# Edge stages of a graph network: the edge product kept as fp32 in SBUF and summed by fp32 matmuls, in place of high and low fp32r parts

## The reference

```
m   = x[src] * rel[edge_type]                       # one row of 256 values for each of 106250 edges
agg = segment_sum((m @ W_half) / deg[dst], dst)     # W_in for the first half of the edges, W_out for the second
x   = x + res * tanh(agg + x @ W_loop + b)
```

## Time and profile before

| | us |
|---|---|
| timed, median of 3 | 2799.92 |
| profiled execution, first to last instruction (its own time; the page lists no other) | 3183.3 |
| edge stage 0 (67 to 1306) | 1239 |
| edge stage 1 (1459 to 2686) | 1227 |
| PE busy | 2759.1 (87%) |
| DVE busy | 2303.9 (72%) |
| ACT busy | 1865.5 (59%) |
| POOL busy | 1952.0 (61%) |

### The profile page before, as it was taken

The page is one execution under the profiler, slowest core; times in us unless marked ns, Lnnn a source line. Parts: engine busy times, 40 slices in busy tenths (PEclk is TensorE's granted clock), DMA queues, the critical chain, the costliest instruction groups (busy, mean ns, idle before and its releaser), DMA issues. The chain is left out here.

```text
span 3183.3 us, 55393 instructions
## 1 busy us (share of the span) xinstructions
PE 2759.1 (87%) x20688; PEld 2587.3 (81%) x20688; DVE 2303.9 (72%) x3258; ACT 1865.5 (59%) x3179; POOL 1952.0 (61%) x2129
## 2 busy tenths in 40 slices
PE   4888888888888888797888888888888887997998
PEld 3888888888888888796877887878777786997998
DVE  6777777777677777896777777777777776995665
ACT  6556665555555555585555555555555554785444
POOL 6666666666666666455666666666666664892223
PEclk9999989999999999899999999999999999998999
DMA  8333333333333333353333333333333333452221
GB/s 259 119 90 89 89 89 90 89 89 90 88 89 90 90 88 90 92 164 104 90 90 90 89 90 92 88 90 90 89 89 92 88 90 98 136 158 90 69 67 64
DMA packets 162458, 312.57 MB, mean 98 GB/s; under 512 B 34061, under 2 KB 95309, under 8 KB 162229
## 3 DMA queue, kind: packets, MB, share of 16 engines
q0 software_dynamic: 79872, 218.21, 23.8%
q1 hardware_dynamic: 81120, 89.89, 8.8%
q10 hardware_dynamic: 1237, 1.41, 0.2%
HBM read 263.90 MB, written 45.48 MB: 97 GB/s over the span
## 5 line engine op out<-in xcount | busy, mean ns | idle before, releaser
L740 PE MATMUL edge_rg<-edge_rel_hi,edge_hot 128*128 128x256 f32 x6656 | 1551.7, 293 | 86.6 <-issue 63.0
L740 PE MATMUL edge_rg<-edge_rel_lo,edge_hot 128*128 128x256 f32 x4992 | 1312.3, 289 | 60.0 <-issue 58.9
L740 PEld LDWEIGHTS edge_rg<-edge_rel_hi,edge_hot 128*128 128x128 f32 x6656 | 1219.6, 197 | 143.7 <-issue 92.2
L548 ACT ACTIVATE edge_hot<-edge_typ,minus_type 128x512 fp32r<-128x512 f32 x832 | 526.8, 685 | 935.9 <-DMA dense_prev<-emb_t 383.9
L740 PEld LDWEIGHTS edge_rg<-edge_rel_lo,edge_hot 128*128 128x128 f32 x4992 | 983.1, 197 | 70.0 <-issue 68.5
L623 DVE TENSOR_TENSOR edge_m_lo<-edge_rg,edge_m_hi 128x1024 fp32r<-128x1024 f32 x416 | 509.3, 1224 | 241.3 <-ACT edge_m_hi L541 127.7
L604 DVE TENSOR_SCALAR edge_hot<-edge_typ,type_of 128x512 fp32r<-128x512 f32 x832 | 582.3, 741 | 12.4 <-ACT edge_hot L548 8.7
L753 PE MATMUL edge_small<-edge_m_hi,edge_sel 128*128 128x258 f32 x1664 | 458.1, 306 | 96.3 <-DVE edge_m_lo L623 90.7
L530 POOL DMA_INDIRECT edge_xg<-emb,src x416 | 399.0, 959 | 225.9 <-issue 96.2
L530 POOL DMA_INDIRECT work<-h,src x416 | 400.7, 963 | 221.9 <-issue 101.9
L530 POOL DMA_INDIRECT edge_xg<-h,src x416 | 400.2, 962 | 216.2 <-issue 102.8
(11 more groups left out here) (183 smaller groups left out, 3933.9 us busy)
## 6 DMA issues: line engine op xcount, KB each, us to landing
work<-emb,src POOLq DMA_INDIRECT x416
edge_xg<-emb,src POOLq DMA_INDIRECT x416
work<-h,src POOLq DMA_INDIRECT x416
edge_xg<-h,src POOLq DMA_INDIRECT x416
set_x_rows<-in_x SPq DMA_DIRECT2D x25, 256.0 KB, 3.9
emb<-set_e_rows SPq DMA_DIRECT2D x25, 256.0 KB, 2.9
emb_t<-acc SPq DMA_DIRECT2D x5, 1280.0 KB
dense_prev<-emb_t SPq DMA_DIRECT2D x25, 256.0 KB, 2.7
```

Of the source, the lines that this page charges most:

```text
L548: act.activation(hot[:, q % 2, c], typ[q % 2][:], ACT.Abs, bias=K["minus_type"][:, c:c + 1]).then_inc(distances, 1)
L740: ins = pe.matmul(rg[q % 2][:, t, :], hot[:, q % 2, c, t * P:(t + 1) * P], part[:, c, :], start=(c == 0 and part is rel_hi), stop=(c == FULL))
```

## The change

The product is written by DVE to SBUF as fp32, into `m`, a ring of four groups; `rg` in PSUM is only read. `m_hi`, `m_lo`, `high` and `low` are gone, and with them `hi_done` and `lo_done`. The selection matrix is fp32 in place of fp32r. PE sums with one fp32 matmul per tile, of 257 columns (256 and one of ones), where it had one of 258 and one of 256 in fp32r. PE's sums wait for `selected`, which DVE sets with the selection matrix, behind the product. The unused way `long()` is changed likewise.

```diff
-        m_hi = s.sb("m_hi", [P, 2, GROUP, DIM + 2], F32R)
-        m_lo = s.sb("m_lo", [P, 2, GROUP, DIM], F32R)
-        sel = s.sb("sel", [P, GROUPS_IN_RING, GROUP * WIN + P - WIN], F32R)
-        sums_sb = s.sb("sums_sb", [WIN, 2, DIM + 2])
+        m = s.sb("m", [P, GROUPS_IN_RING, GROUP, DIM + 1])
+        sel = s.sb("sel", [P, GROUPS_IN_RING, GROUP * WIN + P - WIN])
+        sums_sb = s.sb("sums_sb", [WIN, 2, DIM + 1])
...
-            def high(g, q, i):
-                act.wait_ge(messages, g + 1)
-                act.copy(m_hi[:, q % 2, :, 0:DIM], rg[q % 2][:]).then_inc(hi_done, 1)
...
-                over_groups(act, (0, later(distance)), (2, high), (0, later(one_hot)), (3, copy_sums), (0, clear_one))
+                over_groups(act, (0, later(distance)), (0, later(one_hot)), (3, copy_sums), (0, clear_one))
...
-                dve.tensor_tensor(rg[q % 2][:], xg[q // 2][:, at, :], rg[q % 2][:], ALU.mult).then_inc(messages, 1)
-            def low(g, q, i):
-                dve.wait_ge(hi_done, g + 1)
-                dve.tensor_tensor(m_lo[:, q % 2], rg[q % 2][:], m_hi[:, q % 2, :, 0:DIM].bitcast(F32),
-                                  ALU.subtract).then_inc(lo_done, 1)
+                dve.tensor_tensor(m[:, q, :, 0:DIM], xg[q // 2][:, at, :], rg[q % 2][:], ALU.mult).then_inc(messages, 1)
...
                     select(sel_at(q, 0, GROUP * WIN).rearrange("p (t n) -> p t n", n=WIN),
-                           K["dst_rel"][:, ds(GROUP * g, GROUP)])
+                           K["dst_rel"][:, ds(GROUP * g, GROUP)]).then_inc(selected, 1)
...
-                over_groups(dve, (2, message), (2, one_window), (4, add_window), (2, low), (0, one_hot_later))
+                over_groups(dve, (2, message), (2, one_window), (4, add_window), (0, one_hot_later))
...
-            dve.memset(m_hi[:, :, :, DIM:].bitcast(F32), 0.0).then_inc(filled, 1)
-            dve.wait_ge(filled, 2)
-            dve.memset(m_hi[:, :, :, DIM:DIM + 1].bitcast(F32), 1.0).then_inc(filled, 1)
+            dve.memset(m[:, :, :, DIM:], 1.0).then_inc(filled, 1)
...
-                    pe.wait_ge(lo_done, g + 1)
+                    pe.wait_ge(selected, g + 1)
                     for t in range(GROUP):
-                        lhs = sel_at(q, t, P)
-                        pe.matmul(sums[q // 2][:], lhs, m_hi[:, q % 2, t, :], start=(q % 2 == 0 and t == 0), stop=False)
-                        ins = pe.matmul(sums[q // 2][:, 0:DIM], lhs, m_lo[:, q % 2, t, :], start=False,
+                        ins = pe.matmul(sums[q // 2][:], sel_at(q, t, P), m[:, q, t, :], start=(q % 2 == 0 and t == 0),
                                         stop=(q % 2 == 1 and t == GROUP - 1))
```

More of the change, by code:

```diff
@@ L455, in phase_edges @@
         small = [s.ps(f"small{b}", [P, 512]) for b in range(2)]
-        sums = [v[:, 0:DIM + 2] for v in small]
+        sums = [v[:, 0:DIM + 1] for v in small]
         sums_t = [v[:, 512 - (DC + 1) * WIN:].rearrange("p (k n) -> p k n", n=WIN) for v in small]
@@ L474, in phase_edges @@
         messages = s.sem("messages")
-        hi_done = s.sem("hi_done")
-        lo_done = s.sem("lo_done")
+        selected = s.sem("selected")
         filled = s.sem("filled")
@@ L590, in _ @@
                         clear(c)
-                over_groups(act, (0, later(distance)), (2, high), (0, later(one_hot)), rolled=True)
+                over_groups(act, (0, later(distance)), (0, later(one_hot)), rolled=True)
             with act.Else():
-                over_groups(act, (0, later(distance)), (2, high), (0, later(one_hot)), (3, copy_sums), (0, clear_one))
+                over_groups(act, (0, later(distance)), (0, later(one_hot)), (3, copy_sums), (0, clear_one))
         @block.vector
@@ L597, in _ @@
             dve.memset(rel_sb[:, FULL, :], 0.0).then_inc(rel_zero, 1)
-            dve.memset(sel[:].bitcast(F32), 0.0).then_inc(filled, 1)
+            dve.memset(sel[:], 0.0).then_inc(filled, 1)
             def one_hot(g, q, i):
@@ L689, in all_windows @@
                         add(0, w * WIN, half_at + w * WIN).then_inc(win_added, 1)
-                over_groups(dve, (0, pick_row), (2, message), (2, low), (0, one_hot_later), (3, all_windows),
+                over_groups(dve, (0, pick_row), (2, message), (0, one_hot_later), (3, all_windows),
                             rolled=True)
@@ L732, in relation_rows @@
                     pe.wait_ge(rel_split, 3)
-                    pe.wait_ge(filled, 3)
+                    pe.wait_ge(filled, 2)
                 pe.wait_ge(hot_done, g + 1)
@@ L778, in sum_window @@
                     for k in range(DC):
[L779 to L783, removed]
+                        for t in range(GROUP):
+                            ins = pe.matmul(sums_t[0][:, k, :], m[:, q, t, k * P:(k + 1) * P],
+                                            sel_at(q, t, WIN), start=(t == 0), stop=(t == GROUP - 1))
                     if first:
                         for t in range(GROUP):
-                            ins = pe.matmul(sums_t[0][:, DC, :], K["ones_r"][:], sel_at(q, t, WIN),
+                            ins = pe.matmul(sums_t[0][:, DC, :], K["ones_r"][:].bitcast(F32), sel_at(q, t, WIN),
                                             start=(t == 0), stop=(t == GROUP - 1))
@@ L790, in all_windows @@
                 def all_windows(g, q, i):
-                    wait_apart(pe, lo_done, g + 1, passed)
+                    wait_apart(pe, messages, g + 1, passed)
                     with pe.Fori(0, WINDOWS) as w:
```

## The result

The changed kernel takes 2974.74 us (median of four runs, 2972.66 to 2976.3) against 2800.38 us: the ratio is 1.0619, 95% interval 1.0604 to 1.0634. It is slower by 174 us, where 234 were forecast. The time lies near the low end (2970 us) of the forecast's own range.

What follows compares the result with a forecast made beforehand. The prediction took GpSimd's gathers (5.0 us a group) to bound the timed kernel, with PE close behind. After the change PE's 416 groups of 5.57 us, 2317 us, plus 717 us elsewhere made 3034 us, own range 2970 to 3090.

Steps and rivals of the forecast that it cites:

- GpSimd's floor before: Edge stages before the change: 1664 gathers 1.25 us apart, 2080 us, taken to bound the timed run.
- The fp32 sums: PE's sums: two instructions a call, 0.442 us a tile, weight loads hidden; 1.77 us a group for 0.96, 0.81 more.
- The base of 4.76 us: PE's edge group before the change: 4.76 us of its own work without a gap, read from one undisturbed group.
- the step from the profile to the timed run: Carrying profile readings to timed runs; blamed in advance if the fp32 pitch is 0.22 us and the time still differs.
- DVE and ACT: Edge stages: 1.224 us of DVE and 1.015 us of ACT a group go; neither sets the pace.
- The profiled execution: Whole profiled run after the change: 2317 us PE, 122 us issue waits and 717 us elsewhere, 3156 us or more.
- The timed sum: Timed run after the change: 2317 us of PE in edge stages plus 717 us outside, 3034 us, 234 above the median.
- 1 (stalls that stay, 3137 us): Edge stages: PE plus some 100 us of stalls bound the timed run; all 337 us add, 3137 us; chance 25%.
- 2 (a quicker PE in the timed run): PE's fp32r matmuls start 0.11 us apart when timed; groups 4.40 us before, 5.29 after; 2921 us; chance 9%.
- 3: PE's sums: fp32 instructions stream at the fp32r rate, gathers' floor stands; 2797 us, no change; chance 4%.
- 4: Cheap fp32 sums as in 3, but the product-high-low-sums chain held the timed run; faster, 2722 us; chance 4%.
- 5: PE's sums: fp32 weight loads not hidden, 6.37 us a group; 3367 us; chance 3%.

Runs made afterwards that it cites:

- the second profile: The kernel before the change, unedited, profiled again: one time of 2799.96 us, profile span 2798.0 us.
- 2654.46: Kernel before's PE matmuls without its product-high-low chain: two fp32r sums matmuls a tile (second repeats the product), three gathers a group; 2654.46 us, ratio 0.9473.
- 2455.56: Changed kernel with one fp32r sums matmul a tile (low part left out) and three gathers a group instead of four: 2455.56 us, ratio 0.8765.
- 2704.59: Kernel before the change with three gathers a group in place of four, from a stage's fifth group on: 2704.59 us, ratio 0.9653.
- the run of cut columns: Changed kernel with each fp32 sums matmul but the first of a pair cut into 128 and 129 columns: 2994.61 us.
- the run with one fp32r matmul: Changed kernel with product, selection and sums in fp32r, one matmul a tile, low part left out, four gathers: 2797.18 us, ratio 0.9985.

## Why the prediction was right, and where it was off

*GpSimd's floor before.* Right. The reading of the timed run as 717 us and edge stages at the gathers' floor of 2080, from the pitch of two gathers and a difference of totals, is what the second profile shows directly: 709 us and 2089. The two sides of the maximum each have a run that moves only one of them: gathers taken away help the kernel before by 96 us and the changed one by 0.

*The fp32 sums.* Right in kind, two instructions a call, columns at about half the fp32r rate, loads hidden; and 2% too long in size. A tile's fp32 call in place of one fp32r matmul costs 0.312 us, and a second fp32r matmul costs (2654.46 - 2455.56)/416/4 = 0.12, so the call is 0.312 + 0.12 = 0.43 us where I took 0.442 from a pitch read to two digits. The four passes of the Trainium skill (FP8 and Floating Point Precision, TensorE Precision Notes) gave 0.428 as an estimate: these runs agree, and nearer than my row. The halved rate in the footnote of the Trainium skill's Perfetto Trace Analysis (Engine Utilization) is excluded by the same 0.43 us, if it is read as the cost of a whole call. The exchange (eight fp32r for four fp32 calls) costs (2974.74 - 2654.46)/416 = 0.77 us a group, forecast 0.81.

*The base of 4.76 us.* This step failed. I took the undisturbed group of the earlier trace rows for PE's own work since PE had a record at every moment, and wrote that neither DVE nor ACT sets the pace. It was the loop of product, high, low and one-hots on DVE and ACT. The trace of the kernel before has it around that very group, with both engines:

```profile
378.64 1.22 DVE L617 TENSOR_TENSOR edge_rg<-edge_xg,edge_rg 128x1024 f32<-128x1024 f32 x1
...
379.88 1.02 ACT L541 CAST edge_m_hi<-edge_rg 128x1024 fp32r<-128x1024 f32 x1 [0.77 <-issue]
...
380.94 1.23 DVE L623 TENSOR_TENSOR edge_m_lo<-edge_rg,edge_m_hi 128x1024 fp32r<-128x1024 f32 x1 [0.31 <-issue]
382.08 1.40 DVE L604 TENSOR_SCALAR edge_hot<-edge_typ,type_of 128x512 fp32r<-128x512 f32 x2
383.39 1.22 DVE L617 TENSOR_TENSOR edge_rg<-work,edge_rg 128x1024 f32<-128x1024 f32 x1
```

From product to product it is 4.75 us. PE was stretched to it: its next relation matmul starts 0.05 us after the one-hots end (383.48), and it and the one behind it come 0.24 and 0.22 us after their predecessors, in place of 0.12:

```profile
383.29 0.28 PE L754 MATMUL edge_small<-edge_m_lo,edge_sel 128*128 128x256 f32 x1
383.53 0.39 PE L740 MATMUL edge_rg<-edge_rel_hi,edge_hot 128*128 128x256 f32 x1
383.75 0.28 PE L740 MATMUL edge_rg<-edge_rel_lo,edge_hot 128*128 128x256 f32 x1
```

The two delays, 0.12 and 0.10 us, make up the 0.23 between 4.76 and 4.53 within the rounding of the view. They do not show as idle time because the records of pipelined matmuls, 0.28 us long, overlap. PE's own work was 4.68 in the mean. With 709 us for 717, the error adds up: 8 + 416 x (4.76 - 4.68) + 416 x (0.81 - 0.77) = 8 + 33 + 17 = 58 us of the 59 between 3034 and 2974.7. The prediction had named the step from the profile to the timed run as the one that fails if the pitch is 0.22 and the time still differs; that step held, and PE's base failed in its place.

*DVE and ACT.* The conclusion (their work goes and gives nothing) held for another reason than the one given. They did have a price, the loop at 4.76 us, and it was hidden by the gathers at 5.0. Behind three gathers the loop is worth 50 us, the difference between the runs at 2704.59 and 2654.46.

*The profiled execution.* Forecast 3156 us or more; it was 2973.3, because the issue waits that I carried over from the first profile belonged to that execution and not to the kernel. The timed sum did not use them. Why that execution had them, no run shows.

*The rivals.* 1 (stalls that stay, 3137 us) falls with those waits, which neither the second profile before the change nor the one after it has. 2 (a quicker PE in the timed run) falls: the relation matmuls start 0.12 us apart in profiles whose span equals the timed run. 3 and 4 fall with the pitch of 0.22 us, 5 with the run of cut columns.

## What to carry to other kernels

In a pipeline of engines work moved from one to another is paid by the maximum: here two fp32 tiles of four cost 0 us, the third 46 and the fourth 130, and taking over a quarter of DVE's edge work away gave nothing while the gathers set the pace (the run with one fp32r matmul). Before reading waits from a profile, lay its span beside the timed median; where the two differ by a seventh, use its durations and pitches, and not its waits. A busy engine is not yet the bound: look for a loop over other engines whose period is the same to the digit, and add up its steps.

## What the runs showed of the hardware that was not expected

The first profile of the kernel before had the granted clock at 0.95 over its first edge stage, a mean of its two levels, and PE waiting for "issue"; in the second one, of the same program, the clock is 1.00 and 0.99 in the edge stages, and the relation matmuls are idle for 33 us in all, against 122 us for issue alone. What made the first execution 383 us longer stays open. An fp32 call that follows fp32r ones, and the fp32r one behind it, do not start evenly: the first relation matmul after the sums holds 0.31 us to the next start (2003.19 to 2003.50), while the last fp32 instruction and that matmul start nearly together. Only the sum of both lines can be compared with the other kernel.
